# A language-model tower with 8 experts: the second norm inside the slabs, a folded router, and token lists for the expert tiles

## The reference

```
h = table[x] + bias                                  # embedding rows
h = h + attn(layernorm(h))                           # RWKV-7: a recurrence over time, 4 heads of 64
n = layernorm(h)
x_red = n @ w_red                                    # [2048, 16]
logits = x_red @ (wg / max(|wg|, 1e-4)).T            # [2048, 8]
gates = softmax(logits); idx = argmax(gates); score = max(gates)
o = gelu(n @ W1[idx] + b1[idx]) @ W2[idx] + b2[idx]  # 256 -> 512 -> 256, one expert per token
out = h + o * score
```

## Time and profile before

| | us |
|---|---|
| median of 3 runs | 549.33 (546.82 to 551.17) |
| the profiled execution | 544.08, its span 542.0 |
| busy in the span: PE | 445.7 (82%) |
| DVE | 286.5 (53%) |
| ACT | 200.2 (37%) |
| POOL | 159.4 (29%) |

### The profile page before, as it was taken

One profiled execution on the slowest core, in us unless ns is written; L12 is line 12 of the kernel. 1 busy time (PEld: TensorE's weight loads), 2 busy tenths in 40 slices (PEclk: granted clock), 3 DMA queues, 4 the chain that ended last, 5 costly groups with the idle time before them and its releaser, 6 DMA issues.

```text
span 542.0 us, 23307 instructions
## 1 busy us (share of the span) xinstructions
PE 445.7 (82%) x10731; PEld 352.9 (65%) x10731; DVE 286.5 (53%) x656; ACT 200.2 (37%) x397; POOL 159.4 (29%) x141
## 2 busy tenths in 40 slices
PE   0588999999999999999999987937547999999800
PEld 0457686687787887777786766724324799999700
DVE  2557795865875957857747652135353233222212
ACT  0384744645636637447336320024200222222100
POOL 5736143431523442244313311010055000000073
PEclk9987999999999999999799985767855699999955
DMA  9700000000000000000000000008052276676245
GB/s 302 258 10 3 4 5 4 5 4 6 4 5 4 5 5 4 4 5 5 2 4 5 5 4 5 2 2 310 1 184 98 84 220 212 202 225 200 79 132 178
DMA packets 20810, 37.85 MB, mean 70 GB/s; under 512 B 2800, under 2 KB 14570, under 8 KB 20714
## 3 DMA queue, kind: packets, MB, share of 16 engines
q1 hardware_dynamic: 18378, 30.07, 17.4%
q0 software_dynamic: 2336, 6.30, 3.7%
HBM read 26.14 MB, written 10.22 MB: 67 GB/s over the span
## 4 chain that ended last, share of the span: by engine, by line
PE 74%; DVE 11%; issue 4%; POOL 4%; ACT 3%; DMA 3%; POOLq 0%; DVEq 0%; ACTq 0%
PE ps L1185 8%; PE ps L1196 7%; PE ps L801 6%; PE ps L794 6%; PE ps L904 3%; PE ps L1164 3%; POOL arena L333 3%; PE ps L806 2%; PE ps L1042 2%; PE ps L813 2%; PE ps L880 1%; DVE arena L516 1%; PE ps L1138 1%; PE ps L972 1%; PE ps L845 1%
## 5 line engine op out<-in xcount | busy, mean ns | idle before, releaser
L516 DVE SCALAR_TENSOR_TENSOR arena<-arena 128x256 f32<-128x256 f32 x96 | 47.5, 543 | 6.0 <-PE ps L845 5.0
L1185 PEld LDWEIGHTS ps<-arena 128*128 128x128 f32 x368 | 46.5, 199 | 1.6 <-issue 0.5
L1185 PE MATMUL ps<-arena 128*128 128x128 f32 x368 | 46.8, 282 | 0.1
L333 POOL DMA_INDIRECT arena<-sorted_o,arena x16 | 15.8, 985 | 102.5 <-DMA sorted_o<-arena 98.0
L1196 PE MATMUL ps<-arena 128*128 x184 | 43.5, 380 | 0.1
L475 ACT COPY arena<-ps 128x256 f32<-128x256 f32 x23 | 8.6, 373 | 86.1 <-PE ps L1174 86.1
L794 PE MATMUL ps<-arena 128*128 128x256 f32 x128 | 36.5, 435 | 2.5 <-issue 2.5
L801 PE MATMUL ps<-arena 128*128 128x256 f32 x128 | 36.8, 436 | 1.3 <-ACT arena L452 0.8
L1196 PEld LDWEIGHTS ps<-arena 128*128 128x128 f32 x184 | 33.2, 190 | 4.2 <-issue 0.6
L761 DVE TENSOR_TENSOR arena<-ps,arena 128x512 f32<-128x512 f32 x23 | 15.9, 692 | 35.1 <-PE ps L1185 35.1
L794 PEld LDWEIGHTS ps<-arena 128*128 128x128 f32 x128 | 26.2, 215 | 7.9 <-issue 3.1
(11 more groups left out here) (260 smaller groups left out, 1063.7 us busy)
## 6 DMA issues: line engine op xcount, KB each, us to landing
arena<-W SPq DMA_DIRECT2D x23, 514.0 KB
arena<-W SPq DMA_DIRECT2D x8, 512.0 KB, 6.6
...
arena<-sorted_x SPq DMA_DIRECT2D x23, 128.0 KB, 3.9
sorted_o<-arena SPq DMA_DIRECT2D x23, 128.0 KB, 3.6
out<-arena SPq DMA_DIRECT2D x16, 128.0 KB
...
```

What stands on the lines that cost most here:

```text
L333: pool.indirect_dma_start(out=back[:, t, :], out_offset=None, in_=sorted_o[:, :], in_offset=bass.IndirectOffsetOnAxis(ap=place[:, t:t + 1] ...
L516: last = V.scalar_tensor_tensor(out=mix[j % 3][:, p, :], in0=xx[:, p].rearrange("p b t -> p (b t)"), scalar=mixed_by[MIXES[j]][:, p:p + 1] ...
L1185: last = mm(ps[:, 2 + b, m * 128:(m + 1) * 128], W1_s[q % WB][:, p * HID + m * 128:p * HID + (m + 1) * 128], x_sT[b][:, p, :], start=p == ...
```

## The change

- **Second norm in the slabs.** New steps `N.st`, `N.rs`, `N.lm`, `N.xn` (two turns after a slab's recurrence) do statistics, reciprocal standard deviation and the normalized rows of each slab. ACT writes the normalized rows over `res` (`xn2` is now the same memory), so SP first copies each slab's `res` to a DRAM tensor `kept` and then its `xn2` beside it: a row of `kept` is 2 KB, normalized values and residual. Row 0 of `kept` is zeros.
- **Folded router.** `w_red` times the normalized expert vectors is computed once, early (`E.*` steps, turn 2), as one 256 x 8 matrix `wl`. In the last three turns, steps `R.T0` to `R.T7` (PE transposes, ACT copy) and `R.L0` to `R.L7` (PE product with `wl`; DVE copy, maximum, index, one-hot) do the router a slab at a time.
- **Lists.** The place of a token is split into a tile number and a slot. Two one-hot arrays (`at_slot`, `wanted`) and 16 accumulated PE products give, for each sorted tile and slot, the token's row number and its score.
- **Expert tiles.** POOL gathers 2 KB rows of `kept` by list, four tiles ahead (`XB = 4`), DVE adds `b2` of the tile's expert, multiplies by score and adds the residual, and POOL scatters the finished rows to `out`. Empty slots go to spare rows behind the 2048. The zero fill, the scatter of line 327, the b2 products and the whole gather behind the tiles are removed.
- W2 and b2 are loaded after the first slab, since their memory no longer overlaps that of the attention.

```diff
-WB = 3
+WB, XB = 3, 4
-ORDER = """Q.X0:0 F.xn:2 P.norm:1 O.red:-1 Q.T0:0 P.v:1 Q.X1:0 P.lv:1 Q.T1:0 P.lwa:1 F.xT:2 O.yn:-1 Q.X2:0 P.vga:1 F.xx:2 Q.T2:0
...
+ORDER = """Q.X0:0 F.xn:2 P.norm:1 O.red:-1 R.T0:0 Q.T0:0 P.v:1 R.L0:0 Q.X1:0 P.lv:1 R.T1:0 Q.T1:0 P.lwa:1 R.L1:0 F.xT:2 O.yn:-1 N.st:-2
+Q.X2:0 P.vga:1 R.T2:0 F.xx:2 Q.T2:0 R.L2:0 P.key:1 P.wup:1 Q.W0:0 O.zT:-1 P.lg:1 N.rs:-2 Q.X3:0 R.T3:0 P.cum:1 P.vc:1 N.lm:-2 P.decay:1 N.xn:-2
+R.T6:-1 Q.T3:0 P.rt:1 R.L3:0 Q.A0:0 P.kP:1 P.ar:1 P.tokk:1 P.bP:1 Q.S0:0 R.T4:0 P.k:2 P.M:1 F.stats:3 F.rstd:3 P.q:1 O.out:-1 R.L6:-1 R.L4:0
+Q.W1:0 P.g:1 O.add:-1 R.T5:0 Q.A1:0 P.tokb:1 P.masks:1 Q.S1:0 R.L5:0 O.sq:0 P.r:2 R.T7:-2 R.L7:-2 E.norm:0 E.turn:0 E.fold:0""".split()
+EARLY = 2
@@ SP
-            sp.dma_start(sorted_x.rearrange("(q p) c -> p q c", p=128),
-                         zero_row.unsqueeze(1).broadcast_to([128, SORTED, C])).then_inc(s["cleared"], 16)
-            sp.wait_ge(s["slab_ok"], SLABS)
+            def keep(i):
+                of = kept[1 + i * CH * 128:1 + (i + 1) * CH * 128, :].rearrange("(c p) (w x) -> p c w x", p=128, w=2)
+                sp.wait_ge(s["slab_ok"], i + 1)
+                sp.dma_start(of[:, :, 1, :], res[:, i * CH:(i + 1) * CH, :]).then_inc(s["res_kept"], 16)
+                sp.wait_ge(s["xn2_ok"], i + 1)
+                sp.dma_start(of[:, :, 0, :], xn2[:, i * CH:(i + 1) * CH, :]).then_inc(s["xn2_kept"], 16)
+            keep(0)
             for e in range(E):
-                sp.dma_start(W2_sb[:, e * HC * C:(e + 1) * HC * C], W2[e]).then_inc(s["wexp_in"], 16)
+                sp.dma_start(W2_sb[:, e * HC * C:(e + 1) * HC * C], W2[e]).then_inc(s["w2_in"], 16)
+            sp.dma_start(b2_sb, b2[:, :]).then_inc(s["b2_in"], 16)
+            for i in range(1, SLABS):
+                keep(i)
...
             sp.wait_ge(s["owner_u"], 1)
+            for q in range(SORTED):
                 load_w(q)
@@ POOL
+            def fetch(q):
+                pool.indirect_dma_start(out=x_s[q % XB].rearrange("p w x -> p (w x)"), out_offset=None, in_=kept[:, :],
+                                        in_offset=bass.IndirectOffsetOnAxis(ap=rows_u[:, q:q + 1], axis=0)
+                                        ).then_inc(s[f"xs_in{q % XB}"], 16)
+            pool.wait_ge(s["trash_in"], 16)
+            pool.wait_ge(s["xn2_kept"], 16 * SLABS)
+            pool.wait_ge(s["lists_ok"], 1)
+            for q in range(XB):
+                fetch(q)
+            pool.wait_ge(s["lists_ok"], 3)
+            for q in range(SORTED):
+                pool.wait_ge(s["o2_ok"], q + 1)
+                if q + XB < SORTED:
+                    fetch(q + XB)
+                pool.indirect_dma_start(out=out[:, :], out_offset=bass.IndirectOffsetOnAxis(ap=out_u[:, q:q + 1], axis=0),
+                                        in_=o_s[q % 2], in_offset=None).then_inc(s[f"o_out{q % 2}"], 16)
@@ ACT
+                elif step == "N.rs":
+                    rows = slice(i * CH, (i + 1) * CH)
+                    act.wait_ge(s["mom2_ok"], n)
+                    A.activation(stdev2[:, rows], moments2[:, rows, 1], ACT.Ln, bias=eps_ln).then_inc(s["sd2_ok"], 1)
+                    act.wait_ge(s["sd2_ok"], n)
+                    A.activation(rstd2[:, rows], stdev2[:, rows], ACT.Exp, scale=-0.5).then_inc(s["rstd2_ok"], 1)
+                elif step == "N.xn":
+                    act.wait_ge(s["lessm2_ok"], n)
+                    act.wait_ge(s["res_kept"], 16 * n)
+                    for t in range(i * CH, (i + 1) * CH):
+                        last = A.activation(xn2[:, t, :], res[:, t, :], ACT.Identity, scale=rstd2[:, t:t + 1], bias=less_mean2[:, t:t + 1])
+                    last.then_inc(s["xn2_ok"], 1)
+                elif step[:3] == "R.T" and i == SLABS - 1:
+                    j = int(step[3:])
+                    act.wait_ge(s["xT2_ps"], j + 1)
+                    after(act, "lg2_ps", j - 1)
+                    A.copy(flat(xT2[j % 2]), ps[:, j % 2, :]).then_inc(s["xT2_ok"], 1)
...
+            A.preload_act_table_set("gelu_and_others")
@@ DVE
+                elif step == "N.st":
+                    dve.wait_ge(s["slab_ok"], n)
+                    for t in range(i * CH, (i + 1) * CH):
+                        last = V.bn_stats(stats2[:, t, :], res[:, t, :])
+                    last.then_inc(s["stats2_ok"], 1)
+                    dve.wait_ge(s["stats2_ok"], n)
+                    for t in range(i * CH, (i + 1) * CH):
+                        last = V.bn_aggr(moments2[:, t, :], stats2[:, t, :])
+                    last.then_inc(s["mom2_ok"], 1)
+                elif step == "N.lm":
+                    rows = slice(i * CH, (i + 1) * CH)
+                    dve.wait_ge(s["rstd2_ok"], n)
+                    V.scalar_tensor_tensor(out=less_mean2[:, rows], in0=moments2[:, rows, 0], scalar=-1.0, in1=rstd2[:, rows], op0=ALU.mult,
+                                           op1=ALU.mult).then_inc(s["lessm2_ok"], 1)
+                elif step[:3] == "R.L" and i == SLABS - 1:
+                    dve.wait_ge(s["lg2_ps"], j + 1)
+                    V.tensor_copy(logits[:, rows, :], ps[:, 2 + j % 2, 0:CH * E].rearrange("p (t e) -> p t e", e=E)).then_inc(s["logits_ok"], 1)
+                    dve.wait_ge(s["logits_ok"], j + 1)
+                    for t in ours:
+                        last = V.max(top[:, t, :], logits[:, t, :])
...
+                        last = V.max_index(topi[:, t, :], top[:, t, :], logits[:, t, :])
...
+                    V.tensor_copy(topf[:, rows], topi[:, rows, 0]).then_inc(s["topf_ok"], 1)
...
+                    V.tensor_tensor(onehot[:, rows, :], cst["iota"].unsqueeze(1).broadcast_to([128, CH, E]),
+                                    topf[:, rows].unsqueeze(2).broadcast_to([128, CH, E]), ALU.is_equal).then_inc(s["onehot_ok"], 1)
...
+            V.tensor_scalar(slot_u, place_u, 127, None, ALU.bitwise_and).then_inc(s["route"], 1)
+            V.tensor_copy(slot_f, slot_u).then_inc(s["route"], 1)
+            V.tensor_tensor(first_f, place_f, slot_f, ALU.subtract).then_inc(s["route"], 1)
+            V.scalar_tensor_tensor(out=of_tile, in0=cst["tile_no"].unsqueeze(1).broadcast_to([128, TILES, SORTED]), scalar=128.0,
+                                   in1=first_f.unsqueeze(2).broadcast_to([128, TILES, SORTED]), op0=ALU.mult, op1=ALU.is_equal).then_inc(s["route"], 1)
...
+            V.tensor_tensor(wanted[:, :, 0, :], of_tile, cst["row_no"].unsqueeze(2).broadcast_to([128, TILES, SORTED]), ALU.mult)
...
+            V.tensor_tensor(wanted[:, :, 1, :], of_tile, score.unsqueeze(2).broadcast_to([128, TILES, SORTED]), ALU.mult).then_inc(s["wanted_ok"], 1)
             for t in range(0, TILES, FT):
+                V.tensor_tensor(at_slot[:, t:t + FT, :], cst["slots"].unsqueeze(1).broadcast_to([128, FT, 128]),
+                                slot_f[:, t:t + FT].unsqueeze(2).broadcast_to([128, FT, 128]), ALU.is_equal).then_inc(s["slot_ok"], 1)
+            dve.wait_ge(s["lists_ps"], 1)
+            V.tensor_copy(rows_u, ps[:, 5, 0:SORTED]).then_inc(s["lists_ok"], 1)
...
             def result(q):
                 b = q % 2
+                e = dve.value_load(owner[0:1, q:q + 1], min_val=0, max_val=E - 1)
                 dve.wait_ge(s["o2_ps"], q + 1)
+                V.tensor_tensor(o_b[b], ps[:, 6 + b, 0:C], b2_sb[:, bass.ds(e * C, C)], ALU.add).then_inc(s["ob_ok"], 1)
+                dve.wait_ge(s["ob_ok"], q + 1)
                 if q >= 2:
                     dve.wait_ge(s[f"o_out{b}"], 16 * (q // 2))
-                V.tensor_copy(o_s[b], ps[:, 6 + b, 0:C]).then_inc(s["o2_ok"], 1)
+                V.scalar_tensor_tensor(out=o_s[b], in0=o_b[b], scalar=row_score[:, q:q + 1], in1=x_s[q % XB][:, 1, :], op0=ALU.mult,
+                                       op1=ALU.add).then_inc(s["o2_ok"], 1)
@@ PE
+                elif step[:3] == "R.T" and i == SLABS - 1:
+                    pe.wait_ge(s["xn2_ok"], j + 1)
...
+                    for p in range(2):
+                        for c in range(CH):
+                            last = nc.tensor.transpose(ps[:, j % 2, p * NT + c * 128:p * NT + (c + 1) * 128], xn2[:, j * CH + c, p * 128:(p + 1) * 128], ident)
+                elif step[:3] == "R.L" and i == SLABS - 1:
+                    pe.wait_ge(s["xT2_ok"], j + 1)
+                    for c in range(CH):
+                        for p in range(2):
+                            last = mul(ps[:, 2 + j % 2, c * E:(c + 1) * E], xT2[j % 2][:, p, c * 128:(c + 1) * 128], wl[:, p, :], start=p == 0, stop=p == 1)
...
+            for t in range(TILES):
+                if t % FT == 0:
+                    pe.wait_ge(s["slot_ok"], t // FT + 1)
+                last = mm(ps[:, 5, 0:2 * SORTED], at_slot[:, t, :], flat(wanted[:, t]), start=t == 0, stop=t == TILES - 1)
+            last.then_inc(s["lists_ps"], 1)
```

314 lines of the change are left out of this document (116 added, 198 removed).

## The result

The changed kernel takes 527.0 us (median of 4 runs, 524.1 to 532.1) where the kernel before took 548.1 beside it; the ratio is 0.971 (95% interval 0.965 to 0.976). That is faster, as predicted, but by 21 us and not by 51, and outside the range of 487 to 517. In two later sets, both on one chip, the same kernel took 522.5 and 523.3 us beside 542.0 and 541.7 (ratios 0.964 and 0.951). Ratios and their intervals come from undisturbed executions alone (those at most 1.5% above the fastest of the same kernel), medians and ranges from all, so a ratio can differ from that of two medians, here 0.971 from 0.962.

A forecast was written before the change was run, and what follows sets the result against it. PE fills the slabs and tiles; the change works on the 89.5 us outside them. Terms -2.5 + 1.5 + 3 + 5.9 - 33.8 + 0 - 25.2 = -51.1, from the median 549.33, give 498 us; range 487 to 517.

The forecast's parts named there:

- Step 1: Start: without the zero fill beside the first embedding gathers, the first slab comes earlier; -2.5 us (0 to -3.6).
- Step 2: Norm steps in turns 2 to 6: late inputs cost PE 0.3 us a turn, +1.5 (0 to +6); loads and stores nothing.
- Step 3: Last turn: six R.T and R.L pairs lengthen it, partly offset if the clock holds; +3 us (0 to +9).
- rival B: The clock holds in the last turns, so the pairs there cost 0: -5, 493 us; chance 0.13.
- Step 4: Last two output steps: new norm and router work moves slab_ok from 364.27 to 370.2; +5.9 us (4 to 8).
- Step 5: From last slab's addition to first expert product: 26.2 us in place of 60.03; -33.8 (-30 to -36).
- Step 6: Expert tiles: 4.4 us of slack covers the gathers' 3.5 to 4.0; 0 (0 to +15).
- rival A: Gathers set the pace of the tiles, every second tile waiting 0.9 to 1.5 us; +9 to +14, 509 to 513; chance 0.2.
- Step 7: End: last product to landed scatter takes 4.3 us in place of 29.50; -25.2 (-24 to -26).
- Rival C: Slabs pay more: late inputs +4.5, last turn at half clock +6; 509 us; chance 0.12.
- D: Rival: gathers of 2 KB rows so slow that each tile pair needs 5.9 us more; 555 us; chance 0.03.
- E: Rival: a stall in POOL or SP delays the tile start by all the gain ahead of it; 532 us; chance 0.02.

The follow-up runs named there:

- again: The changed kernel run again unchanged, beside the kernel before: 522.5 us, ratio 0.964.
- allclean: all_repairs with DVE's L707 as a step of its own ahead of the masks, removing the wait of turn 2: 499.8 us.
- the loads alone: Changed kernel with only the W2 and b2 loads moved behind the slabs, after the last keep: 517.3 us, ratio 0.947.
- the pair: Changed kernel with two edits, W2 and b2 loads behind the slabs and second-norm statistics behind the addition: 518.1 us, then 513.2 us (0.946).
- before_w2: Kernel before plus ten 512 KB loads that nothing reads, issued once the second slab was added: 549.0 us beside 543.3, ratio 1.010.
- router_behind: Changed kernel with all R.T and R.L router steps moved from the last turn into the output steps: 509.7 us, ratio 0.937.
- filled_end: Changed kernel with 22 unread products ahead of the list products and SP, not POOL, waiting for the last scatters: 522.8 us, ratio 0.965.
- all_repairs: Changed kernel with all seven repairs (buffers, router, late loads, turn 2's steps, statistics, filler products, SP's end wait): 494.8 us (0.911); again 500.6 us (0.905).

## Why the prediction was wrong

The sum was -51.1; the two profiles give -11.8 (542.0 to 530.2), and -22.6 with the profile of `again` (519.4), nearer to the medians.

| step | predicted | first profile | `again` |
|---|---|---|---|
| 1 and 2, start and turns 2 to 6 | -1.0 | +13.0 | +8.0 |
| 3 and 4, last turn and output steps | +8.9 | +16.8 | +12.3 |
| 5, to the first product | -33.8 | -28.6 | -29.3 |
| 6, tiles | 0 | +7.3 | +6.5 |
| 7, end | -25.2 | -20.2 | -20.1 |

**Step 1** held in kind: the first embedding sum on DVE starts at 12.02 us, not 13.63, 1.6 of the 2.5. By the first output addition nothing of it is left (it starts at 121.2 in `again`, at 121.1 before).

**Step 2 failed.** It priced what DVE adds in a steady turn, and there it was right: turns 4 to 6 take 37.2, 37.3 and 36.9 us in the first profile, no more than the earlier trace rows. What it put at nothing was the load of the 5.2 MB, which comes once. Two other waits, 1.3 us at turn 2's own steps and 1.0 + 0.5 us ahead of `Q.X3` and `Q.T3`, are not shown to be its price: `allclean` gained less than 1 us without the first, and the second comes and goes with the execution, wherever the statistics stand. I had written of the loads that the queues were empty, which is so, and looked for their price at a waiting consumer; it lies in PE's issue, a stall of 1.7 to 2.7 us in all eight profiles with the early loads and in none of ten without them. The two edits together are 7 us of slabs in the mean of the profiles; in time the loads alone (0.947) do as much as the pair (0.946), though the changed kernel itself had 0.964 in one set and 0.951 in another, so that the times settle neither. How much of the 7 us is the stall and how much the half-clock stretches near it stays open, and so does the link that I drew from one to the other: a stretch between 165 and 185 us stands in eight of eight profiles with the big stall and in two of ten without, but `before_w2` has its stretch before its stalls, and `allclean` one at 150 to 160 us without any. The kernel before has one too, at 265 us. The late first addition of the first profile (5.5 us of its +13.0) is not in `again`.

**Step 3 failed in size**: +3 taken, bounds 0 to +9, measured +6.4 to +9.7. What failed is the discount for a clock that would hold: PE was busier than I had counted (40.4 of 43.2 us) and was granted 0.64 all the same, as before, and 0.70 in `again`. The upper bound, +9 where the clock stays at half, was nearly right. That the clock is worth some us here was right as well: in the ten profiles with the pairs in this turn it costs +8.7 to +9.7 at 0.64 to 0.66 and +3.7 and +4.7 at 0.76. So **rival B** (the clock holds) was about the right lever, but the clock didn't hold; that it would have brought this term down to 0 no run shows. **Step 4** was right (+5.9; 22.7 and 23.9 between the last two additions beside 16.8: +5.9 and +7.1). `router_behind` takes steps 3 and 4 back except 2.7, and pays 4 of it in the stage behind.

**Step 5** came 5.2 short. I had DVE pace the lists, 2.5 us for its four operations and 1.1 for PE's last four products; PE paces them, 0.61 + 0.14 + 7.04 = 7.8 in place of 3.6 (+4.2), and even the 4.45 us of `filled_end` are more than DVE's 2.5. The part ahead of the placement is 0.8 longer, since the store of `res` takes 2.85 + 0.44 for my 2.3, and the gathers up to the first product 0.5.

**Step 6 failed, rival A named the right wait**, at half its price and for another reason. (By its own terms, 498 + 9 to 14, it stands at 507 to 512 and not 509 to 513.) I weighed 4.4 us of slack against 3.5 to 4.0 for a gather, with a landing of 2.8 from the earlier trace rows. The landing is 3.3 to 5.4 with a median of 3.7, so need and slack are about even, and each late gather moves the chain `result` to gather to `up_x` of four tiles on. Two more buffers end it (86.8 us). I had added 0.4 for twice the bytes; the rival had the gather suffer from the traffic of W1, which is the side of the Trainium skill (DMA: Bandwidth & Descriptors, "Queues, rings and completion order"), by which queues share the engines packet by packet. The trace separates the two. The first four gathers (419.8 to 424.5 us) move while no other queue moves data, and they land in 3.4 to 3.8 us, median 3.7; the fifteen between 440 and 500 us, beside W1's loads, have a median of 3.6. So the step from 2.8 to 3.7 belongs to these gathers of 2 KB rows, also without other traffic, and the term for them was mis-sized: 0.9 and not 0.4. Only the slow ones among the last five (median 4.7, up to 5.4) are on the side of the rule and of the rival's price. The block of POOL by DVE, weighed there too, could not show: POOL waits for `result` and starts each pair of DMAs behind the new DVE operation (line 785), and in no tile do the two overlap.

**Step 7** was 4.3 us in the sum and is 9.3: the term left out is POOL's closing drain, 5.2. It was in the trace of before, under other work (19.7 us long there, begun while gathers were still to be made, and ended 4.7 us after the last one).

**Rival C** (slabs pay more, +10.5) is what steps 2 and 3 amount to, with a larger sum; D and E did not come. C and A together, which I had as alternatives, come to about 520; with the 5 us each of steps 5 and 7 that is 530, where 527 and 523 were measured. With the seven repairs, most of them an undoing of one named cause each, the kernel takes 494.8 and 500.6 us. That this is the predicted 498 is in part luck: in the profile of `all_repairs` the start and the slabs up to the sixth addition give -2.1 (-1.0 predicted), last turn and output steps +5.3 (+8.9), the stage to the first product -29 (-33.8), the tiles -1 (0) and the end -22 (-25.2). The two large gains stay 8 us short, and payments that the repairs made smaller than predicted make up for most of it.

**Open**: what sets off the half-clock stretches in turns 1 to 3, and whether the statistics' place has any share in them; what delays PE's instructions under traffic (the instruction queues of the profile's queue list are a guess; not tried); how much of the 22 products stood in the last turn's way, and so what a full clock would give there.
